# Late side products evicted ahead of the masks, and routed rows zeroed in twelve pieces instead of five

## What is computed

```python
x = x + tanh(g_xattn[0]) * L0_xattn(ctx, layernorm(x), mask, ...)   # 8 heads of 64, keys = context + latents
x = x + tanh(g_ffn[0])   * L0_ffn(layernorm(x), ...)                # 8 experts, top 2 (mixture of experts)
x = x + tanh(g_xattn[1]) * L1_xattn(ctx, layernorm(x), mask, ...)   # 16 heads of 64
x = x + tanh(g_ffn[1])   * L1_ffn(layernorm(x), ...)                # quantised linear, depthwise conv of 3 taps, silu, quantised linear

# attention (both layers): q from the latents, k and v from [latents, normed context]
sim = where(valid, q @ k.T * scale, -1e30); attn = softmax(sim); out = (attn @ v) @ Wout
# expert layer: every token goes to its two best experts
h = silu(x @ w1[e].T) * (x @ w3[e].T);  y[e] = h @ w2[e].T;  out = sum_e weight[token, e] * y[e]
```

## Time and profile before

| | |
|---|---|
| Median of 3 runs | 1544.02 us (1532.59 to 1547.11) |
| Profiled execution, first to last instruction (span) | 1538.1 us |
| Mean granted TensorE clock in it | 0.937 |
| PE, PE weight load | 1278.3 us (83%), 994.2 us (65%) |
| DVE, ACT, POOL | 1053.8 us (69%), 979.1 us (64%), 1107.9 us (72%) |
| Chain that ended last, by engine | PE 39%, ACT 13%, DVE 12%, POOL 11%, issue 9%, DMA 9% |

### The profile page before, as it was taken

The page is one execution under the profiler, slowest core; times in us unless marked ns, Lnnn a source line. Parts: engine busy times, 40 slices in busy tenths (PEclk is TensorE's granted clock), DMA queues, the critical chain, the costliest instruction groups (busy, mean ns, idle before and its releaser), DMA issues.

```text
span 1538.1 us, 45142 instructions
## 1 busy us (share of the span) xinstructions
PE 1278.3 (83%) x16918; PEld 994.2 (65%) x16918; DVE 1053.8 (69%) x2830; ACT 979.1 (64%) x2319; POOL 1107.9 (72%) x1359
## 2 busy tenths in 40 slices
PE   0778787679878989878999999899999999998852
PEld 0556565557667866656887887667676676766642
DVE  4768788977556656665666666777777777877634
ACT  2778787456455666554656566678777777777631
POOL 4768788687557755466777776788878888787653
PEclk9989999879999989989999999999999999999965
DMA  9599997486999954368999997344555444555310
GB/s 314 134 193 235 246 239 174 83 221 188 218 233 252 233 95 97 73 159 171 247 258 231 269 247 181 79 97 98 105 91 94 90 105 94 106 82 91 79 32 6
DMA packets 438329, 239.96 MB, mean 156 GB/s; under 512 B 388848, under 2 KB 420320, under 8 KB 429024
## 3 DMA queue, kind: packets, MB, share of 16 engines
q1 hardware_dynamic: 408216, 178.51, 55.7%
q10 hardware_dynamic: 26824, 51.22, 10.6%
q0 software_dynamic: 3072, 7.34, 1.6%
HBM read 107.78 MB, written 35.50 MB: 93 GB/s over the span
## 4 chain that ended last, share of the span: by engine, by line
PE 39%; ACT 13%; DVE 12%; POOL 11%; issue 9%; DMA 9%; DVEq 3%; SPq 2%; ACTq 1%; POOLq 0%
PE bank_ring L1088 9%; PE bank_ring L1126 6%; PE bank_ring L1074 5%; PE bank_out L1107 5%; DVE scores L1340 4%; DMA expert_up<-experts_up 4%; ACT scores L849 4%; PE bank_x L1187 3%; POOL probs L654 3%; PE bank_scores L1048 3%; ACT probs L856 3%; PE bank_x L1140 3%; DMA probs_turned<-probs 3%; ACT values L876 2%; DMA context<-in_ctx 2%
## 5 line engine op out<-in xcount | busy, mean ns | idle before, releaser
L654 POOL TENSOR_TENSOR probs<-scores,probs 112x487 f16<-112x487 f32 x384 | 425.0, 1123 | 234.2 <-ACT probs L856 229.1
L849 ACT ACTIVATE scores<-scores,score_min 112x487 f32<-112x487 f32 x384 | 265.8, 693 | 121.0 <-DVE score_min L1340 118.2
L1357 DVE SCALAR_TENSOR_TENSOR values<-bank_ring,values 128x512 f16<-128x512 f32 x192 | 132.4, 689 | 216.4 <-ACT values L876 216.3
L1340 DVE CUSTOM_DVE_ANT_0 scores<-bank_scores,mask 112x487 f32<-112x487 f32 x384 | 238.1, 657 | 2.9 <-PE bank_scores L1048 2.9
L856 ACT ACTIVATE probs<-scores 112x487 f16<-112x487 f32 x384 | 214.2, 604 | 24.4 <-DMA probs_turned<-probs 9.0
L1088 PE MATMUL bank_ring<-weights,kv_B 128*128 128x128 f16 x3072 | 198.3, 223 | 1.2 <-DVE keys L1352 1.2
L876 ACT ACTIVATE values<-bank_ring 128x512 f16<-128x512 f32 x192 | 112.9, 588 | 128.9 <-PE bank_out L1107 125.2
L1088 PEld LDWEIGHTS bank_ring<-weights,kv_B 128*128 128x128 f16 x3072 | 187.2, 100 | 10.5 <-DVE keys L1352 2.0
L1107 PE MATMUL bank_out<-values,probs_turned 128*128 128x64 f16 x4608 | 171.9, 195 | 17.7 <-issue 11.4
L1074 PE MATMUL bank_ring<-kv_B,weights 128*128 128x488 f16 x768 | 181.0, 372 | 0.0
L1107 PEld LDWEIGHTS bank_out<-values,probs_turned 128*128 128x128 f16 x4608 | 160.1, 100 | 21.4 <-issue 14.0
(11 more groups left out here) (230 smaller groups left out, 2470.9 us busy)
## 6 DMA issues: line engine op xcount, KB each, us to landing
expert_up<-experts_up SPq DMA_DIRECT2D x43, 1024.0 KB, 5.5
expert_down<-experts_down SPq DMA_DIRECT2D x43, 512.0 KB, 6.6
raw_weights<-in_weights ACTq DMA_DIRECT2D x8, 1536.0 KB, 10.7
experts_up<-expert_up ACTq DMA_DIRECT2D x8, 1024.0 KB, 4.4
raw_weights<-in_weights ACTq DMA_DIRECT2D x6, 1024.0 KB, 8.0
probs_turned<-probs SPq DMA_TRANSPOSE x384
context_turned_B<-kv_B ACTq DMA_DIRECT2D x16, 375.0 KB, 8.7
kv_B<-context_turned_B ACTq DMA_DIRECT2D x16, 375.0 KB, 3.7
```

The source lines that it names most:

```text
L654: pool.tensor_tensor(PR[:, u % 4, 1, 0:KEYS], S[:, u % 4, 0:KEYS], PR[:, u % 4, 0, 0:KEYS], ALU.subtract).then_inc(probs_split, 1)
L849: act_e.activation(S[:, u % 4, 0:KEYS], S[:, u % 4, 0:KEYS], ACT.Exp, bias=rmin[:, u % 4:u % 4 + 1], scale=-1.0, accum_out=rsum[:, g % 2, ...
L1340: dve.tensor_tensor_reduce(out=S[:, u % 4, 0:KEYS], in0=bS[u % 2][0:TOK, 0:KEYS], in1=mask[:, m, 0:KEYS], scale=1.0, scalar=3.0e38, op0=AL ...
L1357: dve.scalar_tensor_tensor(vN[:, j % 2, 1].rearrange("p t d -> p (t d)"), bank("v", j)[:], 1 / WSCALE, vN[:, j % 2, 0].rearrange("p t d -> ...
```

## The change

VectorE's stream: the call of the late parts moves from behind the masks of step `j+1` to the end of step `j`, behind `split_v(j)` and ahead of the second `gate_hidden`; the next thing in the stream is the masks of step `j+1`. Nothing is added or removed.

SP's stream: the five DMAs that zero the row tables (issued before step -9) become twelve, of at most 4 row slots each, one at the head of steps 2, 4, ... 24, ahead of that step's transposes. They read slots 6 to 9 of `moe_rows`, which are still unused then, and only those are cleared at the start; ACT's wait for the zeroing moves from sequence 0 (step 10) to sequence 6 (step 34).

```diff
--- before.py
+++ after.py
@@ -56,7 +56,10 @@
 TILES = tuple((2 * TOK * (b - a) + EXPERTS * 127) // 128 for a, b in BATCHES)
 SCATTERS = (3, 4)
 XR_SLOTS = 10
-ZERO_DMAS = sum(-(-t // XR_SLOTS) for t in TILES)
+ZERO_SLOT, ZERO_ROWS = BATCHES[0][1], 4
+ZERO_STEP = 2
+ZERO_PIECES = [(b, at, min(ZERO_ROWS, t - at)) for b, t in enumerate(TILES) for at in range(0, t, ZERO_ROWS)]
+ZERO_DMAS = len(ZERO_PIECES)
 
 
 def is_pair(j):
@@ -474,12 +477,10 @@
             sp.dma_start(X[:, 1], x_in[1]).then_inc(x_loaded[1], 16)
             sp.dma_start(X[:, 2:NSEQ], x_in[2:NSEQ].rearrange("n t d -> t n d")).then_inc(x_loaded[2], 16)
             sp.wait_ge(zeros_set, 1)
-            for b in range(2):
-                rows = xs[b].rearrange("(p t) c -> p (t c)", p=128)
-                for at in range(0, TILES[b] * 2 * DIM, XR_SLOTS * 2 * DIM):
-                    n = min(XR_SLOTS * 2 * DIM, TILES[b] * 2 * DIM - at)
-                    sp.dma_start(rows[:, at:at + n], xr[:].rearrange("p s c -> p (s c)")[:, 0:n])\
-                        .then_inc(rows_zeroed, 16)
+
+            def zero_rows(b, at, n):
+                sp.dma_start(xs[b].rearrange("(p t) c -> p t c", p=128)[:, at:at + n],
+                             xr[:, ZERO_SLOT:ZERO_SLOT + n]).then_inc(rows_zeroed, 16)
 
             def load_mask(layer, n):
                 sp.wait_ge(kv_ready[layer if n else 0], n if n or not layer else NSEQ)
@@ -526,6 +527,8 @@
                     .then_inc(turned[u % PT_BUFS], 16)
 
             for j in STEPS:
+                if j >= ZERO_STEP and j % 2 == 0 and (j - ZERO_STEP) // 2 < ZERO_DMAS:
+                    zero_rows(*ZERO_PIECES[(j - ZERO_STEP) // 2])
                 if (j - 3) % 4 == 0 and 0 < (j + 5) // 4 < NSEQ:
                     load_mask(0, (j + 5) // 4)
                 for n in range(NSEQ):
@@ -917,7 +920,7 @@
                 elif name == "m_turn":
                     slot = n % XR_SLOTS
                     act_e.wait_ge(m_normed, n + 1)
-                    if n == 0:
+                    if n == ZERO_SLOT:
                         act_e.wait_ge(rows_zeroed, 16 * ZERO_DMAS)
                     if n >= XR_SLOTS:
                         act_e.wait_ge(scattered[0], 16 * len(scatters(0)))
@@ -1285,7 +1288,7 @@
             for t in (kv[0], kv[1]):
                 for i in range(2):
                     dve.memset(t[:, i, :, :, KEYS:512], 0.0)
-            dve.memset(xr[:], 0.0)
+            dve.memset(xr[:, ZERO_SLOT:ZERO_SLOT + ZERO_ROWS], 0.0)
             dve.memset(mask[:, :, 0:TOK], 0.0).then_inc(zeros_set, 1)
             dve.wait_ge(consts_set, 1)
 
@@ -1658,8 +1661,6 @@
                     mask_scores(2 * j + 1)
                 if is_pair(j + 1) and not halves_in_step(j - 1):
                     split_k(j + 1)
-                for t in late(j - 1):
-                    part(t)
                 for g in range(PAIRS // 4):
                     if slack(g) and j == 4 * g + 6:
                         norm_out(g)
@@ -1728,6 +1729,8 @@
                         norm_out(g)
                 if halves_in_step(j):
                     split_v(j)
+                for t in late(j):
+                    part(t)
                 if m[2]:
                     gate_hidden(m[2][1], m[2][2], m[2][3])
```

## The result

The changed kernel takes **1572.68 us** (median of 4 runs, 1562.05 to 1583.08); the kernel before, run beside it, 1545.57 (4 runs). The ratio is 1.0182, interval 1.0139 to 1.0225: slower, by 28 us. The forecast was 1557 us, 13.5 above before, inside a range of 1536 to 1573. The direction held; the size was half of what came.

A forecast was written before the change was run, and what follows sets the result against it. A ring of VectorE's masks and `split_v` with ScalarE's work was taken as the bound; -10.5 + 4 + 22 - 2 = +13.5 us on 1538.1 gives 1551.6, or 1557 us against the median 5.9 higher; 8 in 10 within 1536 to 1573.

The forecast's parts named there:

- The ring: VectorE's masks, ScalarE's exponentials to values, `split_v`, next masks: late parts inside add 4.45 us a sequence, 2.22 returns.
- ScalarE's 14.9 us of waiting: Steps 112 to 175: ScalarE's values wait 14.9 us for TensorE, 1.86 us a sequence, claimed to go away.
- The start, -10.5: By step 0: the third context lands before VectorE asks, saving 10.5 us, between -8 and -14.
- What is late next is POOL ... 11.2 us: At the start: POOL's first-key mask ends at 32.67, TensorE's first q projection stood at 43.88, leaving 11.2 us.
- The pieces, +4: Steps 2 to 24: zeroing pieces ahead of transposes cost 4 us, bounds 0 and the whole 15 us.
- 3 x 1.4: Steps 2 to 24: about three zeroing pieces fall in piles of DMA traffic, 1.4 us each, +4 us.
- The order, +20: Late parts ahead of the masks: +22 us in steps 105 to 188, -2 us in steps with expert tiles.
- TensorE is the bound: Rival: TensorE's 19.0 us of waits per eight sequences go, the 22 are not paid; -32, 1512 us, chance 0.1.
- The neutral order: Rival: VectorE's late parts and the returned waits cancel, only the start shows; -8, 1536 us, chance 0.17.
- Pieces exposed in full: Rival: DMA bounds steps 2 to 24 and zeroing takes all 15 us; +24, 1568 us, chance 0.15.
- Nothing returned (+44): Rival: none of the 2.2 us a sequence comes back, late parts cost +44; +36, 1580 us, chance 0.05.
- Expert steps: Steps 38 to 56 and 79 to 104: late parts go into VectorE's wait for tanh; -2 us, between -5 and +2.

The follow-up runs named there:

- the pieces alone: Kernel before with only the zeroing changed to twelve pieces in steps 2 to 24, late parts still behind the masks: 1541.39 us, ratio 0.9997.
- the order alone: Kernel before with only VectorE's late parts moved behind `split_v`, ahead of the next masks, zeroing still five DMAs at the start: 1565.13 us, ratio 1.0194.
- the runs ahead of `split_v`: Kernel before with all late parts of step j moved ahead of `split_v(j)`, zeroing as before: 1523.77 us, ratio 0.9878.
- the kernel with `b_lat` alone: Kernel before with only the late part `b_lat` moved ahead of the masks, zeroing as before: 1540.0 us, ratio 0.996.

## Why the prediction was right in sign and half in size

**The ring: right, and sized right in the profile.** From step 105 to step 189 the masks' starts give 502.3 us before and 525.5 after (952.6 to 1478.1), +23.1 against +22. Put in per sequence: 4.65 us against 4.45, because two parts are followed by an issue gap of 0.18 to 0.20 us ahead of the mask (`f_turn` 0.68, `f_rate` 0.46). A sequence got longer by 20.1 / 8 = 2.51 us, so 2.14 came back against 2.22. The forecast's signs came: the 4.94 step is 5.48, the one with the second `f_max` 6.51, the one with `norm_out` shorter. Others were false. TensorE's waits for the latents didn't vanish, and its waits as a whole grew. Nor did all of ScalarE's 14.9 us of waiting go: 3.5 were left.

**Where the size failed.** By the runs, in the prediction's own terms: the start and the pieces, -10.5 and +4, were to give -6.5 us, and the pieces alone show -0.5 (-5.7 to +4.8). The order, +22 and -2, was to cost 20, and alone it costs 29.9 (21 to 38). By the spans, 22.2 us came for 13.5: 3.2 of the 8.7 missing are at the start, 6.5 in steps 0 to 24, and the rest of the span takes 1.0 off.

- *The start, -10.5.* The step that failed is "What is late next is POOL ... 11.2 us". POOL's mask wasn't next, since VectorE's eviction behind the third context waits for POOL's split of the context before (5.91 us, to 35.27), and TensorE's projection gained 7.3 us. All seven kernels with the new zeroing start step 0 earlier by 7.0 to 7.8 us. I had followed the queues of DMA and POOL, and not VectorE's own next instructions.
- *The pieces, +4.* The term "3 x 1.4" was too small: it counted the DMA time of a piece in three piles. Steps 0 to 24 took 10.5 us more in the profile of the change, and step 25 came at 232.6, later than before and not 6 to 8 us earlier. By the runs the pieces took about what the start gave, some 7 us (an estimate: 7.5 - 0.5). How they do it is open, since the longest of the stalls, at step 14, came once without a piece.
- *The order, +20.* Its mechanism is the one forecast, and its profile gives 21.2 us. Why the runs give more is open.

**What stays open.** The runs say that the order alone costs 29.9 us by the ratio and 24.5 by the medians, its profile says 21.2. For the whole change it is 28 us by the ratio (21 to 35) and 22.2 by the spans. The profiled execution of the change is 10.6 us below its median, that of before about 4 (its span is 5.9 us below the median, and in the changed kernel the span is 1.8 us shorter than the time); which stretch the longer executions lose in is in no profile here.

**The rivals.** That TensorE is the bound is refuted: with its bank free earlier the kernel lost 20.1 us in 64 steps. By the rule of the Trainium skill (Perfetto Trace Analysis, Optimization Strategies) the engine that holds TensorE up is the one to work on; the trace of the change disagrees when "work on" means "serve first", and agrees when the eviction is put where it delays nothing, as the runs ahead of `split_v` show, -14.8 us. The neutral order fell with the order alone, +29.9 us. Pieces exposed in full would have made the pieces alone 7.5 us slower (15 less the 7.5 of the start), above their interval, which ends at +4.8. Nothing returned (+44) is refuted by 2.14 us a sequence.

**Expert steps.** -2 was forecast; steps 25 to 104 changed by -0.8 us here and -4.4 with the order alone, within what this stretch varies by: the kernel with `b_lat` alone, the same as before up to step 58, took 6.9 us more from step 25 to step 57. What the order does in the expert steps isn't told apart.

## What to carry to other kernels

Where engines run strictly in order, look for the pair of waits that close a ring (here VectorE's mask to ScalarE, ScalarE's values to VectorE), and price a moved instruction by whether it stands between them: inside, it costs its duration, 0.55 us for 0.53. The place for an eviction is the idle time ahead of the instruction that the ring waits at, not behind it; moving the same call from behind `split_v` to ahead of it turned 1.9% slower into 1.2% faster. When a wait is taken away at the start, read the next ten instructions of the same engine too before looking at the others.

## What was not expected of the hardware

A DMA write of zeros is not free beside transposes: 5.6 MB more in steps 2 to 24 cost about 9.6 us (2 to 18) of the 15 us that the engines need for them. Behind a pile of transfers it is the issuing of transposes that gets long: 15.50 us for two behind 3 MB and one piece, and 14.96 for three around 3 MB without a piece, where two took 2.94 just ahead of the pile in the changed kernel. The stretch with a DMA share over 0.9 isn't reproducible to some us: steps 0 to 24 came out at +0.8 and -3.2 us against before in two kernels with the same instructions there, while steps 112 to 175 agree within 0.8 us for kernels of the same order. The 0.03 us from values to `split_v`, where it waits for them, and the 0.60 or 0.61 from its start to VectorE's next instruction were the same in steps 112 to 175 of every kernel, but for one step of one of them.
